# A token table sent in two transfers, 16-bit one-hot tables, another order in the last block, and other addresses for the expert weights

## The reference

```python
xn = _layernorm(x, axis=-1)
x = x + _L0_attn_ref(xn, ...) + _L0_ffn_ref(xn, ...)

# attention: 16 heads of 16, chunks of 64
q, k, v = (proj(wq), proj(wk), proj(wv))
q = (q @ fq1_w.T + fq1_b) * (q @ fq2_w.T + fq2_b)
k = (k @ fk1_w.T + fk1_b) * (k @ fk2_w.T + fk2_b)
...                     # causal scores inside a chunk, a running k-v state before it
o = o * jax.lax.rsqrt(jnp.mean(o * o, axis=-1, keepdims=True) + EPS) * norm_w
return o @ wo.T

# experts: 8, inner size 512; a token keeps the experts that make up 0.9 of its softmax
probs = jax.nn.softmax(x @ router_w.T, axis=-1)
w = _top_p_weights(probs, TOP_P)
for e in range(n_exp):
    g = jax.nn.silu(x @ gate_w[e].T)
    u = x @ up_w[e].T
    y = g * u @ down_w[e].T
    out = out + y * w[:, e:e + 1]
```

## Time and profile before

| | us |
|---|---|
| median of 3 runs | 874.52 (873.92 to 874.6) |
| the profiled execution | 880.18 |
| its span, first to last instruction | 878.5 |
| PE (TensorE) busy | 784.6 (89%) |
| DVE busy | 526.8 (60%) |
| ACT busy | 389.5 (44%) |
| POOL (GpSimd) busy | 328.6 (37%) |
| mean granted TensorE clock | 0.939 of 2.4 GHz |

### The profile page before, as it was taken

One profiled execution on the slowest core, in us unless ns is written; L12 is line 12 of the kernel. 1 busy time (PEld: TensorE's weight loads), 2 busy tenths in 40 slices (PEclk: granted clock), 3 DMA queues, 4 the chain that ended last, 5 costly groups with the idle time before them and its releaser, 6 DMA issues.

```text
span 878.5 us, 19529 instructions
## 1 busy us (share of the span) xinstructions
PE 784.6 (89%) x6592; PEld 699.6 (80%) x6593; DVE 526.8 (60%) x1170; ACT 389.5 (44%) x909; POOL 328.6 (37%) x366
## 2 busy tenths in 40 slices
PE   5889898989898989945999999999999999999993
PEld 4657676767676767635998999999989999999993
DVE  4567767677767776664456455464464554645642
ACT  3325252535343435333455454464454554644541
POOL 2001010101010101542565665665665655656663
PEclk9969898989899989776999999999999999999997
DMA  2120202020202020430535335353353353443332
GB/s 103 67 73 2 97 0 96 0 96 0 96 0 96 0 72 1 156 50 25 132 54 128 61 54 126 60 127 55 61 127 56 58 127 54 106 83 59 57 58 36
DMA packets 38561, 59.54 MB, mean 68 GB/s; under 512 B 4112, under 2 KB 33808, under 8 KB 37392
## 3 DMA queue, kind: packets, MB, share of 16 engines
q0 software_dynamic: 19776, 27.16, 19.0%
q1 hardware_dynamic: 18768, 32.16, 10.5%
HBM read 37.15 MB, written 22.15 MB: 68 GB/s over the span
## 4 chain that ended last, share of the span: by engine, by line
PE 58%; issue 13%; DVE 9%; DMA 9%; ACT 6%; POOL 4%; POOLq 1%; ACTq 0%; DVEq 0%; SPq 0%
PE A L1049 10%; PE A L1051 9%; PE A L1050 9%; DMA xg<-gather_table,g_idx 6%; PE O L1049 4%; PE O L1051 4%; PE O L1050 4%; PE S L1089 3%; PE A L1280 2%; PE S L1049 2%; PE S L1051 2%; PE S L1050 2%; DMA gather_table<-xna 2%; PE O L1116 2%; ACT xna L541 2%
## 5 line engine op out<-in xcount | busy, mean ns | idle before, releaser
L455 POOL DMA_INDIRECT out<-ybuf,s_idx x98 | 157.7, 1609 | 63.1 <-POOL s_idx L451 46.7
L1049 PE MATMUL A<-gT_hi,w_hi 128*128 128x256 f32 x588 | 167.1, 284 | 6.0 <-issue 4.5
L1050 PE MATMUL A<-gT_lo,w_hi 128*128 128x256 f32 x588 | 166.3, 283 | 0.0
L1051 PE MATMUL A<-gT_hi,w_lo 128*128 128x256 f32 x588 | 166.2, 283 | 0.0
L441 POOL DMA_INDIRECT xg<-gather_table,g_idx x100 | 102.5, 1025 | 113.1 <-ACT w_tok L656 67.5
L356 POOL TENSOR_TENSOR on_lo<-on,on_hi 128x512 fp32r<-128x512 f32 x16 | 20.9, 1305 | 328.7 <-ACT on_hi L511 328.7
L1023 DVE TENSOR_TENSOR h_lo<-h,h_hi 128x256 fp32r<-128x256 f32 x196 | 83.3, 425 | 59.6 <-ACT h_hi L684 59.6
L1049 PEld LDWEIGHTS A<-gT_hi,w_hi 128*128 128x128 f32 x588 | 111.8, 190 | 7.8 <-issue 7.8
L1049 PE MATMUL O<-w_hi,h_hi 128*128 128x256 f32 x392 | 115.4, 295 | 0.0
L1050 PEld LDWEIGHTS A<-gT_lo,w_hi 128*128 128x128 f32 x588 | 111.7, 190 | 0.0
L1051 PEld LDWEIGHTS A<-gT_hi,w_lo 128*128 128x128 f32 x588 | 111.6, 190 | 0.0
(11 more groups left out here) (182 smaller groups left out, 1645.9 us busy)
## 6 DMA issues: line engine op xcount, KB each, us to landing
w_raw<-wffn SPq DMA_DIRECT2D x9, 1536.0 KB, 7.0
gather_table<-xna SPq DMA_DIRECT2D x8, 528.0 KB, 3.0
xa<-x SPq DMA_DIRECT2D x8, 512.0 KB, 3.5
xr<-x SPq DMA_DIRECT2D x8, 512.0 KB, 4.9
out<-yout SPq DMA_DIRECT2D x8, 512.0 KB
out<-ybuf,s_idx POOLq DMA_INDIRECT x104, 3.9
xg<-gather_table,g_idx POOLq DMA_INDIRECT x100
w_raw<-wqk_nat SPq DMA_DIRECT2D x1, 512.0 KB, 5.0
```

The costliest lines, as they stand in the source:

```text
L455: pool.indirect_dma_start(out=out, out_offset=bass.IndirectOffsetOnAxis(ap=s_idx[:, sub:sub + 1], axis=0), in_=ybuf[:, sub, :], in_offset= ...
L1049: mm(out_ap, l_hi, r_hi, start=(k == 0), stop=False)
L1050: mm(out_ap, l_hi, r_lo, start=False, stop=False)
L1051: return mm(out_ap, l_lo, r_hi, start=False, stop=(k == n - 1))
```

## The change

- The table goes out in two transfers: the 256 numbers of a token from `xna` as soon as `norm_apply` has written them (`tokens_out`), and the 8 weights from a tile `wgt` of their own after `choose`, with a semaphore of their own, `wtab_in`. `norm_apply(s + 1)` waits for the first alone.
- `lo_iota`, `hi_iota`, `slot_lo`, `slot_hi`, `oh_hi` become bf16; `slot_lo` and `slot_hi` hold each value twice, so that the comparison's innermost dimension is a pair of neighbouring elements in every operand (`one_hot_rows`). `oh_lo` is made in two instructions of 2048 elements in place of four of 1024.
- In the last block DVE makes `slots` and the first half of `oh_lo` at the end of the first half, ahead of `masked_scores(7, 6)`; ACT makes `oh_rhs` before `head_rstd`; TensorE runs `slot_tokens(7)` before the last `mean_squares`. DVE runs `head_norm(7, 1)` and `add_residual(7)` after the index table.
- The first expert's split moves: ACT's 8 high pieces to its end of the phase, the 8 low pieces from GpSimd to DVE, behind the last `add_residual`. The lines of SyncE quoted above stay as they are.
- A filler of 352 bytes and the second set of weights at the end of phase two's tiles put all four weight buffers at 64 bytes past a multiple of 512; a filler of 480 bytes keeps `gT`, `sg`, `h` at a multiple of 512. The tiles of the first phase that come after move by 32 bytes.

```diff
+            def tokens_out(s):
+                sp.dma_start(table_blk[s][:, :, 0:D], xna[:, :, :]).then_inc(table_in, DMA)
+
             sp.wait_ge(xn_ok, 1)
+            tokens_out(0)
             sp.dma_start(xa[:, :, :], x_blk[1]).then_inc(x_in, DMA)
...
-                sp.dma_start(table_blk[s], xna[:, :, :]).then_inc(table_in, DMA)
+                sp.dma_start(table_blk[s][:, :, D:AUG], wgt[:, :, :]).then_inc(wtab_in, DMA)
                 if not first:
                     sp.wait_ge(y_ok, 2 * s + 2)
                     sp.dma_start(out_blk[s - 1], yout[:, :, :]).then_inc(yout_free, DMA)
+                if not last:
+                    sp.wait_ge(xn_ok, s + 2)
+                    tokens_out(s + 1)
                 if more:
-                    sp.wait_ge(xn_ok, s + 2)
                     sp.dma_start(xa[:, :, :], x_blk[s + 2]).then_inc(x_in, DMA)
...
-                    for piece in range(PIECES):
-                        pool.wait_ge(whi_ok, piece + 1)
-                        low_piece(0, piece * PW)
                     add_zeros(0)
...
-                if last:
-
-                    act.wait_ge(w_in, DMA)
-                    for piece in range(PIECES):
-                        high_piece(0, piece * PW)
...
+                if last:
+                    one_hot_tokens(s)
                 head_rstd(s, 0)
...
-            one_hot_tokens(NBLK - 1)
+            act.wait_ge(w_in, DMA)
+            for piece in range(PIECES):
+                high_piece(0, piece * PW)
...
-                        dve.wait_ge(table_in, DMA * s)
-                    v.tensor_tensor(xna[:, :, D:AUG], pr[:, :, :], keep[:, :, :], ALU.mult).then_inc(w_ok, 1)
+                        dve.wait_ge(wtab_in, DMA * s)
+                    v.tensor_tensor(wgt[:, :, :], pr[:, :, :], keep[:, :, :], ALU.mult).then_inc(w_ok, 1)
...
+            def one_hot_rows(table, numbers, slots2, rows):
+
+                n, m = rows.stop - rows.start, numbers.shape[1] // 2
+                return v.tensor_tensor(
+                    table[:, rows, :].rearrange("p n (m two) -> p n m two", two=2),
+                    numbers[:, :].rearrange("p (m two) -> p m two", two=2).unsqueeze(1).to_broadcast([P, n, m, 2]),
+                    slots2[:, rows, :].unsqueeze(2).to_broadcast([P, n, m, 2]), ALU.is_equal)
+
+            def one_hot(s, part):
+
+                n = TT * NE // 2
+                ins = one_hot_rows(oh_lo, lo_iota, slot_lo, slice(part * n, part * n + n))
+                if part == 1:
                     ins.then_inc(lo_ok, 1)
...
+            def first_low_piece(piece):
+
+                dve.wait_ge(whi_ok, piece + 1)
+                cols = slice(piece * PW, (piece + 1) * PW)
+                v.tensor_tensor(w_lo[0][:, cols], w_raw[:, cols], w_hi[0][:, cols].bitcast(F32),
+                                ALU.subtract).then_inc(wsplit, 1)
...
+                if last:
+                    slots(s, 1, chain)
+                    one_hot(s, 0)
...
                 masked_scores(s, 6)
+                if last:
+                    one_hot(s, 1)
...
-                if last:
-                    slots(s, 1, chain)
-                    one_hot(s, 0)
-                    head_norm(s, 1, chain)
...
+            head_norm(NBLK - 1, 1, chain)
             for i in range(2):
                 add_residual(NBLK - 1, i)
+            for piece in range(PIECES):
+                first_low_piece(piece)
...
+            pe.wait_ge(idx_ok, NBLK)
+            slot_tokens(NBLK - 1)
             pe.wait_ge(ln_o_ok, 2 * NBLK - 1)
             mean_squares(NBLK - 1, 1)
             output_projection(NBLK - 1, 0)
-            pe.wait_ge(idx_ok, NBLK)
-            slot_tokens(NBLK - 1)
```

More of the change, by code:

```diff
@@ L163, in build @@
         lo_i = sb1("lo_i", [P, TT, NE], I32)
-        xna = sb1("xna", [P, TT, AUG])
+        xna = sb1("xna", [P, TT, D])
+        wgt = sb1("wgt", [P, TT, NE])
         xT_hi = sb1("xT_hi", [P, KC, BLK], F32R)
@@ L274, in _, with first_half @@
             sp.dma_start(w_raw[:, :], wffn[0]).then_inc(w_in, DMA)
+            def tokens_out(s):
+                sp.dma_start(table_blk[s][:, :, 0:D], xna[:, :, :]).then_inc(table_in, DMA)
             sp.wait_ge(xn_ok, 1)
+            tokens_out(0)
             sp.dma_start(xa[:, :, :], x_blk[1]).then_inc(x_in, DMA)
-            def first_half(s, first, more):
+            def first_half(s, first, more, last=False):
                 if not first:
@@ L422, in _ @@
             pool.wait_ge(table_in, DMA * NBLK)
+            pool.wait_ge(wtab_in, DMA * NBLK)
             done = pool.alloc_register("tiles_done")
@@ L540, in norm_apply @@
                 for t in range(TT):
-                    last = a.activation(xna[:, t, 0:D], xa[:, t, :], ACT.Identity, bias=nmr_x[:, t:t + 1],
+                    last = a.activation(xna[:, t, :], xa[:, t, :], ACT.Identity, bias=nmr_x[:, t:t + 1],
                                         scale=rstd_x[:, t:t + 1])
@@ L813, in slots @@
                 chain.link(v.tensor_scalar(lo_i[:, :, :], slot_i[:, :, :], P - 1, None, ALU.bitwise_and))
-                chain.link(v.tensor_copy(slot_lo[:, :, :], lo_i[:, :, :]))
-                chain.link(v.tensor_tensor(slot_hi[:, :, :], slot[:, :, :], slot_lo[:, :, :], ALU.subtract))
-                n = TT * NE
-                hi = slot_hi[:, :, :].rearrange("p t e -> p (t e)")
-                v.tensor_tensor(oh_hi[:, :, :], hi_iota[:, :].unsqueeze(1).to_broadcast([P, n, NT // P]),
-                                hi.unsqueeze(2).to_broadcast([P, n, NT // P]), ALU.is_equal).then_inc(slot_ok, 1)
+                twice = lambda a: a[:, :, :].rearrange("p t e -> p (t e)").unsqueeze(2).to_broadcast([P, TT * NE, 2])
+                chain.link(v.tensor_copy(slot_lo[:, :, :], twice(lo_i)))
+                chain.link(v.tensor_tensor(slot_hi[:, :, :], twice(slot), slot_lo[:, :, :], ALU.subtract))
+                one_hot_rows(oh_hi, hi_iota, slot_hi, slice(0, TT * NE)).then_inc(slot_ok, 1)
                 v.tensor_scalar(from_end[:, :], from_end[:, :], float(-BLK), None, ALU.add)
                 chain.link(v.tensor_copy(base[:, 0, :], base[:, TT, :]))
-            def one_hot(s, t):
-                ins = v.tensor_tensor(oh_lo[:, t * NE:(t + 1) * NE, :], lo_iota[:, :].unsqueeze(1).to_broadcast([P, NE, P]),
-                                      slot_lo[:, t, :].unsqueeze(2).to_broadcast([P, NE, P]), ALU.is_equal)
-                if t == TT - 1:
+            def one_hot_rows(table, numbers, slots2, rows):
[8 more added lines that the diff above has]
+                if part == 1:
                     ins.then_inc(lo_ok, 1)
@@ L860, in first_half @@
                 if not first:
-                    one_hot(s - 1, 2)
-                    one_hot(s - 1, 3)
+                    one_hot(s - 1, 1)
                     head_norm(s - 1, 1, chain)
@@ L957, in _ @@
             second_half(NBLK - 1, True, chain)
-            one_hot(NBLK - 1, 2)
-            one_hot(NBLK - 1, 3)
             add_indices(NBLK - 1)
@@ L965, in _ @@
             dve.wait_ge(table_in, DMA * NBLK)
+            dve.wait_ge(wtab_in, DMA * NBLK)
             chain.link(v.scalar_tensor_tensor(idx_f[:, :, :], idx_acc[:, :, 1, :], float(P), idx_acc[:, :, 0, :],
```

23 lines of the change are left out of this document (12 added, 11 removed).

## The result

Before 874.56 us (873.92 to 874.67, 4 runs), after **839.43 us** (837.18 to 841.59, 4 runs): ratio 0.960, 95% interval 0.957 to 0.963. The change makes the kernel 4% faster; forecast were 842.5 us and a range of 831 to 856. The unedited changed kernel, run once more beside the last experiments, took 838.94 us (838.09 to 841.52, 4 runs), ratio 0.957 (0.954 to 0.961).

What follows compares the result with a forecast made beforehand. First-phase blocks were taken as bound by `norm_apply`'s wait for the table's DMA, the second phase by TensorE. -38.3 (stalls) + 5 (clock) + 3.5 (tail) - 2 (addresses) = -31.8, say -32: 874.5 to 842.5 us, range 831 to 856.

Steps and rivals of the forecast that it cites:

- The stall in the loop: First phase: `norm_apply`'s seven waits for the table's DMA go, 5.3 us a block, 6.5 in the first, 38.3 us saved.
- What was added is hidden: First phase: the weights' own transfer and the next tokens' load, about 1.5 us later, delay nothing; 0 us.
- How much of it is tables: Blocks: 16-bit tables relieve DVE of 2.9 us, but only `oh_hi` is on the path, 0.5 us a block within the 5.3.
- the lower bound: DVE's 16-bit table instructions run at the copy's rate: 1.24 us for 2048 elements and 0.70 for `oh_hi`.
- The clock: TensorE before scores 7: a 1.15 us gap lowers the clock in three of seven blocks, 1.7 us each, 5 us back.
- The last block: Tail: the last `out`, queued behind low pieces and 1.5 MB of weights, lands at about 398.9; 3.5 us lost.
- Without this order in the queue the tail would win some 4 us instead: Last block: were the last `out` not queued behind next_weights(1), the tail would gain some 4 us.
- The addresses: Second-phase expert tiles: weights at 64 take the 8.93 us period seen at 32; 25 odd-expert tiles gain 2 us.
- At 64 all four are nearest to 32: Expert weights: the reason given for taking the period of address 32, 8.93 us a tile, for all four buffers.
- The sum: Whole kernel: -38.3 + 5 + 3.5 - 2 = -31.8, say -32 us, giving 842.5 us.

Runs made afterwards that it cites:

- e3: Changed kernel with first-phase tiles and expert weights at their old remainders (32 and 384 by 512): 845.70 us, ratio 0.965.
- e5: Changed kernel with the last `out` issued ahead of next_weights(1) and the eight low pieces ahead of the last two add_residual: 831.53 us, ratio 0.950.
- e6: Changed kernel with only DVE's low pieces moved ahead of the last two add_residual, SyncE's order as changed: 833.77 us, ratio 0.951.
- e8: Changed kernel with only the four expert weight tensors back at remainders 32 (even) and 384 (odd) by 512: 845.13 us, ratio 0.964.
- e11: Changed kernel with the last `out` issued first and expert weights at remainders 0 (even) and 256 (odd): 842.40 us, ratio 0.959.
- e12: Changed kernel with the last `out` issued first and expert weights at remainders 128 (even) and 192 (odd): 832.15 us, ratio 0.948.
- e14: Changed kernel with the last `out` issued first and all four expert weight tensors at remainder 192: 827.96 us, ratio 0.946.
- e10: Changed kernel with tables, iotas and slot halves in 32 bits again (`oh_lo` result stays 16 bits): 851.13 us, ratio 0.971.
- e1: Kernel before with only the table's transfer split in two; 32-bit tables, old last-block order and old addresses: 848.75 us, ratio 0.969.
- e4: Changed kernel with the last `out` issued ahead of next_weights(1) in SyncE's queue, nothing else: 828.84 us, ratio 0.946.
- e2: Kernel before with only the 16-bit tables, `oh_lo` in two halves; one transfer, old order and addresses: 877.19 us, ratio 0.999.

## Why the prediction came out right, and where its terms were off

**The stall in the loop: right.** Predicted were 5.3 us a block and the projections at 190.8; measured 44.4 - 39.2 = 5.2 in a middle block and 31.8 in six blocks together (from the first block's projections to scores 4 of the last block, 294.3 us before and 262.5 after), with TensorE waiting for DVE's mask of scores 6, the engine that was named as late next. For the first block 6.5 were predicted: from scores 5 to the first projection it took 14.37 us before (48.48 to 62.85) and 8.05 after (45.50 to 53.55), so 6.3. The first block gave 3.0 more ahead of its stall, because two low stretches of the clock, at 17.5 to 20.5 and 27.5 to 31 us (0.50 and 0.52 before), were missing in after's profiled execution (1.00). e3, e5, e6, e8, e11, e12 and e14 show their second `norm_apply` at 41.5 to 42.6 in place of 39.8, with one or both of these low stretches back: by all that differs between these kernels an accident of an execution, about 2 us that the change can't claim. The four executions of e12 alone had mean clocks of 0.965 to 0.979 and took 837.1 to 829.9 us.

**What was added is hidden: right.** The weights' transfer, for which no row had a price, lands in 1.8 us, and nothing in the loop waits for it. The next tokens land 5.5 to 7.0 us after their issue in place of 3.5 to 3.7, 2 us more or over that where 1.5 were forecast, and nothing waits for them either.

**How much of it is tables: mis-sized.** I put the tables on the path by `oh_hi` alone, 0.5 us a block, and let the rest "cost or give nothing". e10 gives 1.07 us a block (40.27 against 39.2) and e1 1.15: DVE's shorter first half also brings `slot` forward, for which TensorE's `slot_tokens` otherwise waits (0.31 us in e1). The split is then worth 4.05 and not 4.8. The two errors cancel in the sum, which is luck: the 5.3 us came out right, their division did not. The instruction times were right at the lower bound: 1.22 and 0.69 us measured, 1.24 and 0.70 taken. The Trainium skill (VectorE: DVE Perf Modes, "The perf-mode tier table") gives 1.22 us for 2048 elements of bf16; the trace agrees, 1.22.

**The clock: this term was wrong.** I gave 5 us back, three falls in seven blocks behind a gap of 1.15 us. The gap is 0.72, and in the ten profiled executions with 16-bit tables and the split transfer none of 68 such gaps (0.54 to 0.74 us) has a fall behind it. The mechanism exists, though: where the tables are 32 bits wide the gap is 1.23 us in most blocks, and the clock fell behind it in two of seven blocks of e1 and in two of seven of e10, 1.5 us each. So the price of a fall (1.7 predicted) was nearly right, the length of the gap and hence the count were not. The 16-bit tables keep the gap at a length behind which no fall was seen. That it's the gap's length that decides is argued and not shown: ten of the fourteen blocks with the longer gap had no fall.

**The last block: right, in each step.** By scores 4 of the last block as a mark, predicted against measured, in before's times: last `mean_squares` 375.7 and 374.7, end of `add_residual` 387.3 and 386.2, issue of the weights 391.1 and 389.9, `out` landed 398.9 and 398.5, loss 3.5 and 3.6 us. "Without this order in the queue the tail would win some 4 us instead": e4 wins 9.2 - 3.6 = 5.6. The queue is what the forecast made of it, seen in e4 and e6. The Trainium skill (DMA: Bandwidth & Descriptors, "Two DMAs through the same engine are not ordered") says that within one queue of one DMA engine descriptors start in order but are pipelined; the trace agrees: `out` took 8.1 us behind the weights and 2.9 without them, and landed 1.3 us behind the weights (357.3 and 356.0), less than it takes alone.

**The addresses: right in sign, too small.** 2 us were taken, from the period of 8.93 seen at 32. At 64 the period is 8.87 in both kinds of expert: 25 x 0.14 + 24 x 0.06 = 4.9 us. Measured are 4.7 (e8, 458.9 to 454.2) and, in the median, 5.7 to 6.3 (e8, e3 against after, with 2 and 3 us of it at the start of the profiled executions). "At 64 all four are nearest to 32" was the step that failed: nearness in address says nothing, since 0 is as near as 64 and is the slowest of all. The Trainium skill (SBUF — State Buffer, "Who interferes with whom") has TensorE wait for no other engine, and the prediction drew a price of 0 for the addresses from it; e3 and e8 measured 4.7 to 4.8 us in the tiles, so that price was wrong. Whether ports have a part in it no run shows.

**The sum.** Against the profiled executions: -41.2 measured, -31.8 predicted. Of the 9.4 us between them, 5 are the clock term, 3.0 the start of the first block and 1.8 the tiles (458.0 - 454.2 against the 2 taken); the stalls gave 38.1, 0.2 less than forecast. Between the medians the change is -35.1 against a forecast of -32: before's profiled execution lay 5.7 us above its median, after's 0.4 us below its own, so a part of the 9.4 isn't in the medians. Before's had a mean clock of 0.939, below all 46 of its runs beside the experiments (0.941 to 0.956). So it is partly luck that 842.5 and 839.4 are so close: the clock term was 5 us too dear, and the profile from which the stalls were read made the gain 6 us too large.

What stays open: why the remainder matters to TensorE. It matters where the weights are stationary and where they are moving, but no run moves one operand of the two alone, and none explains why tiles of one expert differ at 64.

## What to carry to other kernels

- Before an instruction is sped up, look at which engine has no gap in that stretch: the same 16-bit tables gave nothing beside the stall (e2), and 12 us once the stall was gone and the last block reordered (e10). Test an edit in the kernel as it will be.
- A small transfer that others wait for belongs ahead of a large one in its queue, and what gates the large one must not gate the small one: two lines of order were 10 us here, as much as the tables gave in the loop (9.8, e10).
- Where TensorE is busy throughout, try a few places of its operands, here between 0 and 384 bytes past a multiple of 512; it costs a filler tensor. Best measured version: e4, with 64 or 192 alike.

## What the runs showed of the hardware

- The pace of the same fp32 products depended on the remainder of the weights' address by 512: steady tiles of 9.07 us at 0 and 256, 8.98 to 9.01 at 384, 8.98 at 128, 8.92 to 8.96 at 32, 8.73 to 8.92 at 64, 8.62 to 8.93 at 192.
- A two-input VectorE comparison of 2048 elements took 2.29 us with 32-bit inputs (e10) and 1.22 with 16-bit ones (after), although the inner dimension was only a pair and the one around it had step 0 for one input.
- TensorE's granted clock stayed at 1.00 behind 68 gaps of 0.54 to 0.74 us, fell behind 4 of 14 gaps of 1.03 to 1.23 (e1, e10), at the gap of 2.08 us in the first block of all 14 profiled executions, and in all 14 blocks with the stall of 2.7 to 3.9 (before, e2). Kernels with the same code in their first 60 us showed or lacked low stretches there: they reached scores 4 of the last block between 316.1 and 321.4 us (e4 and e5 differ only behind 300 us: second `norm_apply` at 40.0 and 41.7).
